# First attention: half of the next tile's key projection between two sets of transposes, and GpSimd's weight parts behind the key root

## What is computed

```python
x = x + L0_attention(layernorm(x), ctx)      # one head, 64 keys per batch
x = x + L0_sparse_ffn(layernorm(x))
x = x + L1_attention(layernorm(x), ctx)      # 32 heads, 8 key/value heads
x = x + L1_ffn(layernorm(x))
```

```python
features_n = rmsnorm(features, fn_w)
Q = jnp.einsum('btd,fd->btf', text, Wq_w) + Wq_b
K = jnp.einsum('bsd,fd->bsf', features_n, Wk_w) + Wk_b
Q = rmsnorm(Q, qn_w)
K = rmsnorm(K, kn_w)
scores = jnp.einsum('btf,bsf->bts', Q, K) * scale
attn = jax.nn.softmax(scores, axis=-1)
attended = jnp.einsum('bts,bsf->btf', attn, features_n)
```

## Time and profile before

| | us |
|---|---|
| median of three runs | 1486.43 |
| profiled execution, its own time | 1488.97 |
| its span in the trace | 1487.2 |
| TensorE busy | 1456.9 (98%) |
| VectorE busy | 1121.6 (75%) |
| ScalarE busy | 793.4 (53%) |
| GpSimd busy | 708.2 (48%) |

### The profile page before, as it was taken

One profiled execution on the slowest core, in us unless ns is written; L12 is line 12 of the kernel. 1 busy time (PEld: TensorE's weight loads), 2 busy tenths in 40 slices (PEclk: granted clock), 3 DMA queues, 4 the chain that ended last, 5 costly groups with the idle time before them and its releaser, 6 DMA issues.

```text
span 1487.2 us, 27765 instructions
## 1 busy us (share of the span) xinstructions
PE 1456.9 (98%) x9948; PEld 851.1 (57%) x9948; DVE 1121.6 (75%) x2161; ACT 793.4 (53%) x3201; POOL 708.2 (48%) x668
## 2 busy tenths in 40 slices
PE   8999999999999989999999999999999999999998
PEld 6888645555555555556555555655555565555554
DVE  5887787888877878676776776777677677677868
ACT  5678731211123776565556646655754664565663
POOL 6678885554665453344233434333343433343553
PEclk9999999999999999999999999999999999999999
DMA  5744445443444585534443543543454345234523
GB/s 191 239 150 141 128 90 116 106 94 82 75 82 72 118 167 90 125 86 76 110 79 66 108 99 54 102 89 78 89 93 89 82 84 106 51 66 70 103 48 114
DMA packets 359225, 148.98 MB, mean 100 GB/s; under 512 B 342336, under 2 KB 342720, under 8 KB 356144
## 3 DMA queue, kind: packets, MB, share of 16 engines
q1 hardware_dynamic: 357792, 139.87, 44.2%
q10 hardware_dynamic: 1296, 7.34, 1.5%
HBM read 60.11 MB, written 4.19 MB: 43 GB/s over the span
## 4 chain that ended last, share of the span: by engine, by line
PE 49%; DVE 6%; ACT 5%; POOL 3%; DMA 2%; SPq 1%; issue 1%; DVEq 0%; POOLq 0%; ACTq 0%
PE bank L72 16%; PE bank L73 15%; PE bank L74 15%; ACT a_prob L1977 3%; PE bank L2649 2%; DMA a_kT_lo<-a_kn_lo 2%; ACT a_oT_lo L1954 1%; POOL a_qrs L1849 1%; DVE a_oT_lo L2246 1%; ACT a_qr_hi L1951 1%; POOL a_prob L1831 1%; DVE a_kn L2201 1%; DVE a_qve L2185 1%; DVE x_res L2169 1%; DVE x_res L2333 1%
## 5 line engine op out<-in xcount | busy, mean ns | idle before, releaser
L1977 ACT ACTIVATE a_prob<-a_prob,a_nmx 128x64 f32<-128x64 f32 x512 | 170.2, 334 | 250.0 <-DVE a_nmx L2222 249.9
L1831 POOL TENSOR_TENSOR a_prob<-a_prob,a_mask 128x512 f32<-128x512 f32 x64 | 79.9, 1269 | 278.4 <-DVE a_prob L2216 278.4
L72 PE MATMUL bank<-w,xT_hi 128*128 128x448 f16 (+1 forms) x512 | 187.5, 366 | 1.1 <-PEq L1043 1.1
L74 PE MATMUL bank<-w,xT_hi 128*128 128x448 f16 (+1 forms) x512 | 187.3, 366 | 0.0
L73 PE MATMUL bank<-w,xT_lo 128*128 128x448 f16 (+1 forms) x512 | 187.2, 366 | 0.0
L1849 POOL TENSOR_TENSOR a_qrs<-a_qve,neg_half 128x8 f32<-128x8 f32 x64 | 104.2, 1645 | 138.9 <-DVE a_qve L2185 138.6
L1251 ACT CAST f_h_hi<-h 128x448 f16<-128x448 f32 x64 | 35.6, 563 | 207.2 <-DVE h L1325 207.1
L2169 DVE SCALAR_TENSOR_TENSOR x_res<-bank,a_oinv,x_res 128x512 f32<-128x512 f32 x128 | 95.4, 746 | 64.2 <-PE bank L74 64.2
L2174 DVE SCALAR_TENSOR_TENSOR a_qr_lo<-bank,a_qr_hi 128x512 f16<-128x512 f32 x128 | 87.9, 687 | 46.4 <-ACT a_oT_lo L1954 27.4
L1837 POOL TENSOR_TENSOR a_p_hi<-a_prob,a_rden 128x512 f16<-128x512 f32 x64 | 69.5, 1086 | 104.3 <-DVE a_rden L2230 104.3
L1189 POOL TENSOR_TENSOR f_h_lo<-h,f_h_hi 128x448 f16<-128x448 f32 x64 | 72.8, 1141 | 88.9 <-ACT f_h_hi L1251 88.9
(11 more groups left out here) (355 smaller groups left out, 4439.3 us busy)
## 6 DMA issues: line engine op xcount, KB each, us to landing
shared<-in_l_wq SPq DMA_DIRECT2D x8, 1024.0 KB, 4.9
shared<-in_l_wo SPq DMA_DIRECT2D x8, 1024.0 KB, 5.2
shared<-in_w ACTq DMA_DIRECT2D x8, 896.0 KB, 4.7
craw<-in_w SPq DMA_DIRECT2D x11, 512.0 KB, 3.8
a_wide<-in_l_ctxT SPq DMA_DIRECT2D x16, 256.0 KB, 4.0
x_res<-in_x SPq DMA_DIRECT2D x16, 256.0 KB, 4.4
shared<-in_ctx SPq DMA_DIRECT2D x16, 256.0 KB, 4.3
shared<-in_l_wkv SPq DMA_DIRECT2D x8, 512.0 KB, 4.0
```

The source lines that it names most:

```text
L72: pe.matmul(out, a_hi, b_hi, start=first, stop=False)
L74: return pe.matmul(out, a_hi, b_lo, start=False, stop=last)
L1831: pool.tensor_tensor(blocks(prob[u][:, :]), blocks(prob[u][:, :]), mask[:, :].unsqueeze(1).broadcast_to([P, NB, S]), ALU.add).then_inc(s_m ...
L1977: ins = act.activation(pt, pt, ACT.Exp, bias=nmx[:, col:col + 1], accum_out=den[:, col:col + 1])
```

## The change

TensorE: in bodies 1 to 13 the first two steps (k = 0, 1; six matmuls) of the key projection of tile n + 2 are issued between `q_T(n + 1)` and `k_T(n + 1)`, behind a wait for the bias sum of tile n + 1's keys, whose bank they overwrite. The next body begins with the last two steps. In body 1 the whole projection of tile 2 is still there, since only body 1 begins to work ahead.

GpSimd: `split_w1` moves from behind `weigh` to behind `key_root`, ahead of the wait for L696, in bodies 8 to 13; in body 14 it moves ahead of that wait; body 15 has no key root, and its place is the same.

```diff
--- before.py
+++ after.py
@@ -432,17 +432,16 @@
             if project:
                 if not first:
                     key_root(n + 1)
+            if n - 1 in SPLIT_AT:
+                split_w1(SPLIT_AT[n - 1])
+            if project:
                 pool.wait_ge(s_kn, n + 2)
             if n == ROOT_AT:
                 prep.pool_rstd(pool, 0)
-            if n == NT - 2:
-                split_w1(SPLIT_AT[n - 1])
             if project:
                 features_lo(n + 1)
             if ahead:
                 weigh(n + 2)
-            if n - 1 in SPLIT_AT and n != NT - 2:
-                split_w1(SPLIT_AT[n - 1])
             if n == C_AT:
                 split_c1()
             if n == C_AT + 1:
@@ -922,7 +921,7 @@
 
         def body(n, first=False, ahead=True, project=True):
             if project and not first:
-                project_k(n + 1)
+                project_k(n + 1, ks=range(2, KD) if n > 1 else range(KD))
                 project_q(n + 1)
             pe.wait_ge(s_kTl, n + 1)
             if not first:
@@ -946,6 +945,9 @@
                 q_T(1)
             elif project:
                 q_T(n + 1)
+                if ahead:
+                    pe.wait_ge(s_kb, n + 2)
+                    project_k(n + 2, ks=range(0, 2))
                 k_T(n + 1)
             if n in PREP_AT:
                 t = PREP_AT[n]
```

## The result

| | before | after |
|---|---|---|
| median of five runs, us | 1486.43 (1485.33 to 1488.51) | 1497.02 (1496.05 to 1498.44) |
| profiled execution, its own time, us | 1488.97 | 1498.44 |
| its span, us | 1487.2 | 1496.6 |
| mean granted clock | 0.999 | 0.996 |

After to before is 1.0067, with a 95% interval of 1.0053 to 1.0081: the change costs 10.6 us by the medians, 9.4 by the spans of the two profiled executions. The forecast was 1495.1 us in a range of 1491.0 to 1498.5.

A forecast was written before the change was run, and what follows sets the result against it. In the first attention TensorE waits for the scaled keys, 4.7 us in 6 waits. Interval changes sum to +8.7 us on the profiled 1488.97, giving 1497.7; that execution lay 2.5 above the median, so 1495.1 us, range 1491.0 to 1498.5.

The forecast's parts named there:

- the hold: First attention: VectorE's scaling of the keys waits 1.71 us for GpSimd's weight part, lasting about 2.46 instead of 0.75.
- K(8): Start of body 8's key transposes; with the scaling held, the interval since body 7's grows by 1.71 us.
- K(9): Start of body 9's key transposes; interval since body 8's 10.83 us against 9.19, +1.64.
- K(10): Start of body 10's key transposes; gain and delay cancel, interval since body 9's 10.20 us against 10.36, -0.16.
- K(11): Start of body 11's key transposes; interval since body 10's 10.68 us against 9.39, +1.29.
- K(12) and K(13): Starts of the key transposes in bodies 12 and 13; intervals 11.23 us against 9.51 and 9.52, +1.71 each.
- K(5): Start of body 5's key transposes, late by VectorE's weight maxima; half projection ahead shortens the interval 9.43 to 8.97, -0.46 us.
- The end of the stage: Body 14, no second projection to fill in: scaling ends at 9.42 us against 8.19, delaying the last scores, +1.23.
- VectorE is first: Rival: in the first attention VectorE's scaling starts before GpSimd's weight part, which waits 0.6 us; -1.7, 1484.7 us, chance 0.06.
- All is covered: Rival: the 1.38 us of moved matmuls buy off each key-transpose wait up to that size; -5.5, 1480.9 us, chance 0.03.

The follow-up runs named there:

- the GpSimd part alone: Kernel before with only the GpSimd move (weight parts directly behind the key root), later stages' DMA transposes as plain copies: 1488.81 us, ratio 1.0012 to the kernel before.
- The TensorE part alone: Kernel before with only the half key projection moved ahead, later stages' DMA transposes as plain copies: 1480.87 us, ratio 0.9962 to the kernel before.
- the control: Kernel before with the later stages' DMA transposes turned into plain copies, first attention untouched: 1480.36 us, ratio 0.9957 to the kernel before.
- the weight part behind the scaled keys: Changed kernel, plain copies in later stages, weight part moved one line, behind GpSimd's wait for the scaled keys: 1481.86 us, ratio 0.9964 to the kernel before.
- the run with writes alone: Changed kernel, plain copies in later stages, each weight part done as two memsets instead of the subtraction: 1480.52 us, ratio 0.9952 to the kernel before.
- the change with plain copies: Changed kernel with the later stages' DMA transposes turned into plain copies: 1489.89 us, ratio 1.0021 to the kernel before.

## Why the prediction was right, and by how much it was off

- **The mechanism** is shown. The weight part goes first and the scaling waits, in all seven bodies; taking away its reads alone, or its place alone, takes the hold away, and the GpSimd part alone brings 7.0 of the 7.35 us at `k_T(15)`. The hold was put at 1.71 us and is 1.62: the weight part is 0.03 us shorter than the 1.92 of the sum, and the scaling's work starts 0.20 us before the weight part's recorded end, where L2234 had 0.14. The signs came true in the main: the scaling lasts about 2.4 us in seven of 16 (2.36 to 2.38 in six of them, 2.21 in body 9, where VectorE came later) and the weight part stays at 1.9; the matmuls wait for the scaling for 9.2 us and not for over 10.
- **The intervals**, in the order of the sum (forecast, then measured): K(8) 11.36, 11.26; K(9) 10.83, 10.07; K(10) 10.20, 10.10; K(11) 10.68, 10.58; K(12) and K(13) 11.23, 11.12 each. Five of the six are 0.10 or 0.11 us low, which is the hold's 0.09. The reading that K(10)'s gain and hold cancel held.
- **K(9), mis-sized by 0.76 us.** The step was the root at K(8) + 8.28, "set by VectorE's long row". That row had a hold in it that the prediction did not see, and GpSimd's own row was just as late. VectorE and GpSimd, before:

```profile
110.15 1.90 POOL L456 TENSOR_TENSOR w<-shared,w 128x896 f16<-128x896 f32 x1
...
111.33 0.75 DVE L108 TENSOR_SCALAR ln_nm<-ln_mv 128x4 f32<-128x4 f32 x1
...
113.48 1.30 POOL L416 TENSOR_TENSOR a_big<-a_wide,a_big 128x512 fp32r<-128x512 f32 x1
```

and after:

```profile
113.21 0.17 DVE L108 TENSOR_SCALAR ln_nm<-ln_mv 128x4 f32<-128x4 f32 x1
...
114.51 1.30 POOL L416 TENSOR_TENSOR a_big<-a_wide,a_big 128x512 fp32r<-128x512 f32 x1
```

A 128x4 operation (L108) lasts 0.75 us beside the weight part of that body; in the kernel after it is alone and takes 0.17, so all that VectorE and ScalarE do behind it for the root comes some 0.6 us earlier after K(8). GpSimd's last step ahead of the key root (L416) ended at K(8) + 7.35; without the weight part ahead of the tile roots it ends at K(8) + 6.50. Both had to come forward for the root to end at K(8) + 7.60. Moving the weight part did not only make a collision, it also ended one.
- **K(5), wrong in sign.** The step was -0.46 us; it is +0.54 (9.97 against 9.43). The chain did start elsewhere, but the change brought the copy of the weight maxima forward onto a GpSimd step that reads SBUF, and the copy lost about 1 us there. Also, `k_T` now stands behind `q_T` and the half projection: `q_T` waited 0.79 us for the query bias sum, and `k_T` followed 1.89 us after it. The 7.16 us at which `q_T` is wanted were in the prediction, but were not applied to this body. The TensorE part alone shows the same, the GpSimd part alone doesn't (36.31 us from `k_T(2)` to `k_T(6)`, as in the control).
- **The end of the stage.** From K(13) to the last scores +1.23 was forecast and +1.01 measured (12.64 against 11.63).
- **The clock, not in the sum at all**: +2.8 us (6.34 against 3.54). Without it the last scores are 7.9 us late (174.94 against 167.03), 0.8 less than forecast; with it the last probability transpose is 10.7 late (181.28 against 170.57), 2.0 more. By the profiles it is the step that puts the time above 1495.1 (by 1.9 us). That the forecast is this near is partly luck: the 0.8 us too much ahead of the last scores make up for a part of the 2.8 us left out. The profile of before might have warned me: with waits of 1.5 us where TensorE has no second projection to fill in, the forecast itself had made TensorE idle where it used to be busy. The 2.5 us by which the profiled execution of before lay above the median are likely in part the fall at 538 us, which the prediction did not look at.
- **The range** is 0.6 us wider at the top than its own terms give: 1495.1 + 7 x 0.21 + 1.3 is 1497.9. The measured 1497.02 lies within either.
- **The rivals.** "VectorE is first" has not come, and no run made it come. Its working was right in one place, though: with no hold, the TensorE part alone loses 0.65 us at K(9), since the query bias sum starts 7.23 us after K(8); forecast +0.6 from 7.24. "All is covered" is refuted by that same run: 4.7 us of waits were bought off, and the time stayed.

What stays open: what decides whether the clock falls at the end of the stage; whether filling TensorE's waits in the last two bodies with idle transposes would keep the clock up (by the numbers above, worth about 3 us to the changed kernel and to the one with the weight part behind the scaled keys); whether one small GpSimd operation ahead of the weight part would let VectorE go first; and whether the half projection in the late bodies alone, where it doesn't meet the copy of the weight maxima, is worth the 0.5 us by which it shortens the way from `k_T(14)` to the last scores (11.10 against 11.63). None of these was tried. No version measured here beats the kernel before: the best ones are the same as their control within the intervals.

## What to carry to other kernels

An idle gap on one engine is not free room when another engine works in just that gap: before moving work into it, look at what the operations read. Of two operations that hold each other up, the later one here took nearly the sum of both times (2.37 us for 1.89 and 0.75), and the one that started a few hundredths of a microsecond earlier went first; here a move by one line, to the other side of a wait, decides over 8 us. And a wait can cost twice, once as itself and once through the matmul clock behind it: in five of the six profiles with a wait of 1.8 us ahead of the last scores the clock fell.

## What the runs showed of the hardware

- A GpSimd subtraction of two SBUF operands (128x896, 1.89 us) holds VectorE's scaling of two SBUF operands (128x512) from 0.75 to 2.37 us; two GpSimd memsets in its place (0.84 us each) don't: 0.75 us. The Trainium skill, "SBUF — State Buffer", "Who interferes with whom", says that a VectorE instruction with two SBUF inputs contends with a GpSimd instruction that reads SBUF, "not with one that only writes it"; the run with writes alone agrees.
- By the same section of the Trainium skill the later instruction waits for all of the first, which would be 1.82 us in body 8 (106.88 to 108.70); the trace has 1.62, so 0.2 us of it overlap by the records, in all bodies alike.
- Short VectorE operations are held just as well, and are easily overlooked: a copy 128x256 goes from 0.29 to 1.28 us, a 128x4 operation from 0.17 to 0.75 us. The same section of the Trainium skill names copies and operations with a scalar as a case of its own, with conditions on their operands that no run here tests.
- TensorE's clock fell to 0.50 around the wait of 1.8 us at the end of the stage in the kernel after, in the change with plain copies, in the GpSimd part alone, and in both kernels whose hold was gone (writes only, behind the scaled keys); in the TensorE part alone it stayed at 1.00 behind a wait of the same length, and in the control behind one of 1.37 us. These are single executions, and by the mean clocks the fall is missing in some others of the same kernels. What decides isn't settled. The way from the last scores to the last probability transpose took 3.54 us without a fall, and 5.04, 5.92, 6.34, 6.44 and 6.53 us with one.
